# Routing tables of a two-layer MoE kernel: one-hot tables with the pair index innermost, in two-byte numbers, built on VectorE

## The chip, the cores and the metric

One core of a Trainium2 chip. Its engines run side by side, each with a queue of its own: TensorE (PE; PEld is its weight load), VectorE (DVE), ScalarE (ACT), GpSimd (POOL) and SyncE (SP, which here only issues DMAs). The metric is the device time of one launch in microseconds. Every stretch below is one core's.

## The reference, cut to what matters

The input is x of shape (4, 24, 16, 256): 1536 tokens of 256 numbers. There are two layers. Each adds an attention-like mixer to x, normalises the tokens, and adds a mixture of eight experts of which every token uses two. Layer 1 differs from layer 0 in its gates, width and activation.

```python
router = softmax(xf @ gate_w + gate_b)
k_scores, k_idx = top_k(router, 2)
comb = zeros((t, 8)).at[arange(t)[:, None], k_idx].add(k_scores)
for i in range(8):
    h = silu(xf @ w1[i] + b1[i])
    out = out + (h @ w2[i] + b2[i]) * comb[:, i:i + 1]
```

The kernel computes each expert only for the tokens that chose it, so it needs lists: which tokens go to which expert, and with which gate.

## The kernel before, in words

**Work and order.** Tokens lie in 12 tiles of 128 (token = tile x 128 + partition). A token and its first or second choice form a pair; each partition holds 24 pairs (PAIRS = 2 choices x 12 tiles). Per layer the order is: normalise, transpose, scores and values (the value products are in `values`, L1133, through `product`, L1097 to L1099; their weights are `xnT_hi` and `xnT_lo`, taken every 16th element), projection, second normalise, gates (`route`), the routing tables, and then a loop over blocks of 128 gathered token rows, 24 to 31 of them, each for one expert (`step`, L1306). Each engine has its own hand-written program; semaphores order them. PE runs filler matmuls in its waits (`keep_busy`, L1101).

**The routing tables.** DVE turns the gates into a slot number for each pair (L922 to L963). The slot's low seven bits are its row in a block (`rowblk[:, 0]`), the rest its block (`rowblk[:, 1]`); `rowblk` is four-byte. Then two one-hot tables are made:

- `blk_hot` (L967) has, for each pair, a one at its block out of TAB = 32. `onehot_blk` holds five products of it: with the token number within the tile (L972, DVE), with the tile's first token (L555, `blk_value` at L310, POOL) and with three parts of the gate (L590 on POOL for two of them, L1031 on DVE for the third).
- `onehot_row` (L976) has, for each pair, a one at its row out of 128. It takes one tensor_scalar for each of the 24 pairs, comparing `iota_bf` (0 to 127, two-byte) with that pair's row.

PE multiplies them, pair by pair, into PSUM: 24 matmuls of 64 columns give the token list (L1242), and 24 of 96 columns the gate list (L1324). The weights are a pair's 128 rows, the moving columns its blocks. In both tables the pair index is outside, so that a matmul reads packed numbers. PE starts the first list in four groups of six pairs (ROW_CHUNKS), each when DVE has made its six rows (`hot_rows`).

**What hangs on them.** From the first list DVE makes `gather_tab` (L983 to L985), POOL issues `gather(0)` (L571), and when the rows have landed PE transposes them (L1256), ACT and DVE split them in a high and a low part (L721, L1016), and PE makes `first_product(0)`. Behind that on PE come the 24 matmuls of the gate list, then `step(0)`. DVE meanwhile does the block arithmetic (L1034 to L1052), reads the gate list (L1056 to L1058) and enters its loop. POOL makes its two gate products between `gather(0)` and `gather(1)`. Between the first list and the first gathered block PE runs 12 fillers (BUSY_GATHER), before it 16 (BUSY_LIST).

**Memory.** `region_a` is used anew by each stage; during the tables `h_sb`, `hT_hi` and others share its place, since they are first written later. ACT's queue around the mixer's end is: copies of `outT` (L674), the cast of the biases (L680, waits for their load), a table load (L682), then the high parts of an expert's weights (L624) for POOL's subtractions (L544).

Of the kernel before, what the change touches and what calls it, by code (L numbers as in the profile page):

```python
# [15 lines left out]
BF16 = mybir.dt.bfloat16  # L16
I32 = mybir.dt.int32
ALU = mybir.AluOpType
# [3 lines left out]
P = 128  # L22
# [3 lines left out]
TILES = TOKENS // P  # L26
# [6 lines left out]
E, TOPK = 8, 2  # L33
PAIRS = TILES * TOPK
# [5 lines left out]
TAB = MAX_BLOCKS + MAX_BLOCKS % 2  # L40
ROW_CHUNKS = 4

# [23 lines left out]
class LayerSems:  # L66


    def __init__(self, sem, L):
# [46 lines left out]
        self.hot_blk = sem(f"hot_blk_{L}")  # L116
        self.tab_mm = sem(f"tab_mm_{L}")
# [29 lines left out]
def metaformer(nc, x, conv_w, ffn_w, out):  # L147

    with ExitStack() as ctx:
        def sb(name, shape, dt=F32):  # L150
            return ctx.enter_context(nc.sbuf_tensor(name, shape, dt))

        def sem(name):
            return ctx.enter_context(nc.semaphore(name))
# [13 lines left out]
        with nc.sbuf_tensor("onehot_blk", [P, PAIRS, 5, TAB], BF16) as onehot_blk:  # L168
            pass
# [3 lines left out]
        xT_lo = sb("xT_lo", [P, KC, P], F32R)  # L173
        h_sb = sb("h_sb", [P, 1024])
        blk_hot = sb("blk_hot", [P, PAIRS, TAB], BF16)
# [4 lines left out]
        onehot_row = sb("onehot_row", [P, PAIRS, P], BF16)  # L180
# [58 lines left out]
        rowblk = sb("rowblk", [P, 2, PAIRS])  # L239
# [28 lines left out]
        tile_first = sb("tile_first", [P, TILES])  # L268
        iota_bf = sb("iota_bf", [P, P], BF16)
# [38 lines left out]
        def blk_value(eng, v, value):  # L308

            return eng.tensor_tensor(onehot_blk[:, :, v, :].rearrange("p (k i) b -> p k i b", k=TOPK),  # L310
                                     blk_hot[:, :, :].rearrange("p (k i) b -> p k i b", k=TOPK),
                                     value.unsqueeze(3).to_broadcast([P, TOPK, TILES, TAB]), ALU.mult)
# [154 lines left out]
        def _(pool):  # L467
            cc = [0]

            def made(ins):  # L470
                cc[0] += 1
                ins.then_inc(made_seq, 1)
                pool.wait_ge(made_seq, cc[0])
# [21 lines left out]
            for L in range(2):  # L495
# [16 lines left out]
                for q in range(PIECES * SLOTS):  # L512
                    if L == 0 and q == PIECES:
# [10 lines left out]
                        made(pool.tensor_copy(tile_first[:, :], token_i[:, :]))  # L524
                        made(pool.iota(token_i[:, 0:1], pattern=[[0, 1]], base=1, channel_multiplier=1))
                        made(pool.tensor_copy(token_id[:, :], token_i[:, 0:1]))
                        made(pool.tensor_copy(iota_bf[:, :], iota_i[:, :]))
# [10 lines left out]
                    if q == 2 * PIECES:  # L538
# [14 lines left out]

                pool.wait_ge(s.blk_hot, 1)
                blk_value(nc.gpsimd, 1, tile_first[:, :].unsqueeze(1).to_broadcast([P, TOPK, TILES])  # L555
                          ).then_inc(s.hot_blk, 1)
                pool.wait_ge(s.hot_blk, 1)
# [30 lines left out]
                pool.wait_ge(s.blk_hot, 2)  # L588
                for v in range(2):
                    blk_value(nc.gpsimd, 2 + v, gate_part[:, v, :, :]).then_inc(s.hot_blk, 1)  # L590
                    pool.wait_ge(s.hot_blk, v + 2)
# [17 lines left out]
        def _(act):  # L609
            for L in range(2):  # L610
# [61 lines left out]
                for j in range(0, 8, 2):  # L672
                    act.wait_ge(s.oT_mm, j + 1)
                    nc.scalar.copy(outT[:, j // 4, :, 4 * (j % 4):4 * (j % 4) + 4].rearrange("p n q -> p q n"),  # L674
                                   bank[4 + j % 4][:, 0:4 * BN].rearrange("p (q n) -> p q n", q=4)).then_inc(s.o_act, 1)

# [90 lines left out]
        def _(dve):  # L767
            nc.vector.memset(busy_in[:, :], 0.0).then_inc(busy_ready, 1)
            for L in range(2):
# [165 lines left out]
                if L == 0:  # L935
# [31 lines left out]
                nc.vector.tensor_tensor(blk_hot[:, :, :],  # L967
                                        iota[:, 0:TAB].unsqueeze(1).to_broadcast([P, PAIRS, TAB]),
                                        rowblk[:, 1, :].unsqueeze(2).to_broadcast([P, PAIRS, TAB]),
                                        ALU.is_equal).then_inc(s.blk_hot, 1)  # L970
                dve.wait_ge(s.blk_hot, 1)
                nc.vector.tensor_scalar(onehot_blk[:, :, 0, :], blk_hot[:, :, :], token_id[:, :], None, ALU.mult  # L972
                                        ).then_inc(s.hot_rows, 1)
                dve.wait_ge(s.y_mm, 6)
                for j in range(PAIRS):
                    hot = nc.vector.tensor_scalar(onehot_row[:, j, :], iota_bf[:, :], rowblk[:, 0, j:j + 1], None,  # L976
                                                  ALU.is_equal)
                    if (j + 1) % (PAIRS // ROW_CHUNKS) == 0:
                        hot.then_inc(s.hot_rows, 1)
# [51 lines left out]
                blk_value(nc.vector, 4, gate_part[:, 2, :, :]).then_inc(s.hot_rows, 1)  # L1031


# [60 lines left out]
        def _(pe):  # L1094
# [16 lines left out]
            for L in range(2):  # L1111
# [126 lines left out]
                pe.wait_ge(s.hot_blk, 1)  # L1238
                for j in range(PAIRS):
                    if j % (PAIRS // ROW_CHUNKS) == 0:  # L1240
                        pe.wait_ge(s.hot_rows, j // (PAIRS // ROW_CHUNKS) + 2)
                    mm = pe.matmul(bank[5][:, 0:2 * TAB], onehot_row[:, j, :],  # L1242
                                   onehot_blk[:, j, 0:2, :].rearrange("p v b -> p (v b)"),
                                   start=(j == 0), stop=(j == PAIRS - 1))
# [76 lines left out]
                pe.wait_ge(s.hot_blk, 3)  # L1321
                pe.wait_ge(s.hot_rows, ROW_CHUNKS + 2)
                for j in range(PAIRS):
                    mm = pe.matmul(bank[6][:, 0:3 * TAB], onehot_row[:, j, :],  # L1324
                                   onehot_blk[:, j, 2:5, :].rearrange("p v b -> p (v b)"),
                                   start=(j == 0), stop=(j == PAIRS - 1))
# [39 lines left out]
```

## Time and profile before

| what | value |
|---|---|
| median of 3 runs | 665.55 us (664.88 to 667.18) |
| span of the profiled execution | 669.3 us; no other time of that execution is given |
| PE, DVE, ACT, POOL busy | 600.0, 339.2, 278.0, 283.5 us |
| DMA | 59.89 MB, mean 89 GB/s |
| mean granted clock of PE | 0.943 of full |

Busy time is what an engine spends in instructions, not how well it uses them. A line of a timeline gives the start, the time from the first start to the last end, the engine, the line of the kernel, the output, the inputs and a count. [...]

### The profile page before, as it was taken

How to read it: one execution, taken by the hardware profiler on the slowest of the kernel's cores; microseconds unless marked ns; L12 is line 12 of the kernel's file. 1: busy time of each engine (PE TensorE's matmuls, PEld its weight loads, DVE VectorE, ACT ScalarE, POOL GpSimd, SP SyncE). 2: the span in 40 equal slices, each digit the busy share in tenths (PEclk: the TensorE clock that was granted, in tenths of full speed). 3: DMA queues.
4: the chain of work that ended last, by engine and by line, in shares of the span. 5: the costliest groups of instructions: out<-in, count | busy, mean ns of one | idle time of the engine just before them, and what ended most of it. 6: DMA issues, size and time to landing. Idle time of an engine off the chain costs nothing.

```text
span 669.3 us, 15565 instructions
## 1 busy us (share of the span) xinstructions
PE 600.0 (90%) x3942; PEld 514.9 (77%) x3943; DVE 339.2 (51%) x745; ACT 278.0 (42%) x528; POOL 283.5 (42%) x309
## 2 busy tenths in 40 slices
PE   8898837999999999999869985689999999999992
PEld 4797614879888898897549774269999999999982
DVE  6635797454232643442186376744465555553330
ACT  5376522544333643443064736022344354432220
POOL 4948334254343434343354536223433543344332
PEclk9799968999999999999879996779999999999995
DMA  6423780264212521243203059302153552121111
GB/s 228 127 64 101 243 299 17 67 180 102 39 31 36 153 39 31 36 103 88 78 21 124 18 165 305 91 16 34 30 160 91 139 118 39 24 32 31 31 28 16
DMA packets 41418, 59.89 MB, mean 89 GB/s; under 512 B 5072, under 2 KB 34816, under 8 KB 41392
## 3 DMA queue, kind: packets, MB, share of 16 engines
q1 hardware_dynamic: 30448, 45.39, 21.4%
q0 software_dynamic: 10944, 14.17, 12.6%
q8 instruction: 14, 0.23, 0.2%
q14 instruction: 12, 0.10, 0.1%
HBM read 46.96 MB, written 13.63 MB: 91 GB/s over the span
## 4 chain that ended last, share of the span: by engine, by line
PE 74%; DVE 13%; DMA 4%; issue 4%; ACT 1%; DVEq 1%; ACTq 1%; POOL 0%; SPq 0%; POOLq 0%
PE bank L1097 17%; PE bank L1099 17%; PE bank L1098 17%; PE bank L1288 6%; PE bank L1273 4%; PE bank L1176 2%; PE bank L1256 2%; PE bank L1209 2%; DVE stats L780 2%; DVE onehot_row L976 2%; PE bank L1153 1%; PE bank L1198 1%; DMA expert_io<-xn_dram,gather_tab 1%; DMA xres<-in_x_dram 1%; PE bank L1105 1%
## 5 line engine op out<-in xcount | busy, mean ns | idle before, releaser
L1097 PE MATMUL bank<-w_hi,xT_hi 128*128 x336 | 139.7, 416 | 0.0
L1097 PE MATMUL bank<-w_hi,hT_hi 128*128 (+1 forms) x392 | 117.2, 299 | 5.9 <-DVE hT_lo L1069 5.9
L1099 PE MATMUL bank<-w_hi,xT_lo 128*128 x336 | 115.5, 344 | 0.0
L1098 PE MATMUL bank<-w_lo,xT_hi 128*128 x336 | 115.5, 344 | 0.0
L1098 PE MATMUL bank<-w_lo,hT_hi 128*128 (+1 forms) x392 | 112.2, 286 | 0.0
L1099 PE MATMUL bank<-w_hi,hT_lo 128*128 (+1 forms) x392 | 112.1, 286 | 0.0
L1069 DVE TENSOR_TENSOR hT_lo<-bank,hT_hi 128x512 fp32r<-128x512 f32 (+1 forms) x112 | 64.7, 619 | 63.8 <-ACT hT_hi L742 32.5
L742 ACT CAST hT_hi<-bank 128x512 fp32r<-128x512 f32 (+1 forms) x112 | 54.3, 536 | 99.0 <-PE bank L1288 98.9
L1097 PEld LDWEIGHTS bank<-w_hi,hT_hi 128*128 128x128 f32 (+1 forms) x392 | 76.4, 195 | 8.3 <-issue 7.6
L571 POOL DMA_INDIRECT expert_io<-xn_dram,gcol x58 | 59.0, 1017 | 47.2 <-POOL gcol L567 36.9
L544 POOL TENSOR_TENSOR w_lo<-raw,w_hi 128x1024 fp32r<-128x1024 f32 (+1 forms) x24 | 56.9, 2396 | 50.5 <-ACT w_hi L624 50.5
L1098 PEld LDWEIGHTS bank<-w_lo,hT_hi 128*128 128x128 f32 (+1 forms) x392 | 76.5, 195 | 0.0
L1099 PEld LDWEIGHTS bank<-w_hi,hT_lo 128*128 128x128 f32 (+1 forms) x392 | 76.5, 195 | 0.0
L582 POOL DMA_INDIRECT mid_dram<-expert_io,scol x28 | 44.8, 1601 | 72.4 <-DVE expert_io L1087 71.5
L1025 DVE TENSOR_TENSOR w_lo<-raw,w_hi x40 | 48.9, 1240 | 46.0 <-ACT w_hi L730 45.0
L582 POOL DMA_INDIRECT out_dram<-expert_io,scol x28 | 44.9, 1603 | 61.9 <-DVE expert_io L1087 59.9
L1097 PEld LDWEIGHTS bank<-w_hi,xT_hi 128*128 128x128 f32 x336 | 65.8, 196 | 3.3
L1099 PEld LDWEIGHTS bank<-w_hi,xT_lo 128*128 128x128 f32 x336 | 63.9, 190 | 4.8
L1098 PEld LDWEIGHTS bank<-w_lo,xT_hi 128*128 128x128 f32 x336 | 64.7, 193 | 3.8
L1273 PE MATMUL bank<-bias_rows,expert_sel 96*128 96x336 bf16 (+1 forms) x168 | 57.6, 343 | 3.0 <-DVE xT_lo L1016 3.0
L721 ACT CAST xT_hi<-bank 128x256 fp32r<-128x256 f32 x58 | 21.5, 370 | 93.2 <-PE bank L1256 93.1
L752 ACT ACTIVATE h_sb<-bank 128x512 f32<-128x512 f32 x56 | 33.6, 600 | 53.5 <-PE bank L1099 53.5
(200 smaller groups left out, 1030.8 us busy)
## 6 DMA issues: line engine op xcount, KB each, us to landing
raw<-in_L_ffn_w_dram SPq DMA_DIRECT2D x32, 512.0 KB, 4.1
raw<-in_L_ffn_W_dram SPq DMA_DIRECT2D x16, 672.0 KB, 4.0
raw<-in_L_ffn_W_dram SPq DMA_DIRECT2D x16, 336.0 KB, 4.6
xn_dram<-raw SPq DMA_DIRECT2D x6, 512.0 KB, 3.7
xres<-in_x_dram SPq DMA_DIRECT2D x3, 512.0 KB, 4.6
wqkv<-in_L_conv_W_qkv_dram SPq DMA_DIRECT2D x2, 768.0 KB, 7.4
mid_dram<-xres SPq DMA_DIRECT2D x3, 512.0 KB, 5.6
xres<-mid_dram SPq DMA_DIRECT2D x3, 512.0 KB, 4.9
```

What stands on the lines that cost most here:

```text
L544: pool.tensor_tensor(w_lo[:, e, at], raw[:, 0, at], w_hi[:, e, at].bitcast(F32), ALU.subtract).then_inc(s.pool_split, 1)
L571: pool.indirect_dma_start(out=xg, out_offset=None, in_=xn_dram, in_offset=bass.IndirectOffsetOnAxis(ap=rows, axis=0)).then_inc(s.gathered, 16)
L582: pool.indirect_dma_start(out=acc, out_offset=bass.IndirectOffsetOnAxis(ap=scol[:, :], axis=0), in_=y_sb, in_offset=None, bounds_check=TOK ...
L742: nc.scalar.copy(hT_hi[0:f.kh, half * j:half * (j + 1), :], bank[4 + j][0:f.kh, 0:half * P].rearrange("p (k s) -> p k s", s=P)).then_inc(s ...
L752: nc.scalar.activation(h_sb[:, f.chunk * j:f.chunk * (j + 1)], bank[j][:, 0:f.chunk], ACT.Silu).then_inc(s.h, 1)
L1025: nc.vector.tensor_tensor(w_lo[:, slot, at], raw[:, (q // PIECES) % 2, at], w_hi[:, slot, at].bitcast(F32), ALU.subtract).then_inc(s.w_lo, 1)
L1069: nc.vector.tensor_tensor(hT_lo[0:f.kh, part, :], bank[4 + j][0:f.kh, 0:half * P].rearrange("p (k s) -> p k s", s=P), hT_hi[0:f.kh, part, ...
L1097: pe.matmul(out, hi, w_high, start=first, stop=False)
L1098: pe.matmul(out, hi, w_low, start=False, stop=False)
L1099: return pe.matmul(out, lo, w_high, start=False, stop=last)
L1273: pe.matmul(bank[n][:, 0:f.chunk], expert_sel[:, e, :], bias_rows[:, cs], start=True, stop=False)
L1288: mm = pe.transpose(bank[4 + j][0:f.kh, k * P:(k + 1) * P], h_sb[:, o:o + f.kh], ident[:, :])
```

## The change

Both tables get the pair index innermost, and all compared and multiplied numbers two bytes. An `iota_rep` (each of 0 to 127, six times over) is written once per layer by ACT. It lies where `h_sb` lies later. The block table and the products run over 768 contiguous elements. `onehot_row` is made by four tensor_tensor operations of 128 x 6 elements instead of 24 tensor_scalar operations. All products of `blk_hot` move to DVE; those that POOL made, with its waits, go. The tile product stands ahead of the row tables on DVE, the three gate products stand together behind `xT_low(0)`. PE waits for both value products ahead of the first list, and for all five ahead of the second; the matmuls read one pair with a step of 6 elements (weights) or 24 (columns). The number of matmuls and their sizes stay.

```diff
+PER_CHUNK = PAIRS // ROW_CHUNKS
-        with nc.sbuf_tensor("onehot_blk", [P, PAIRS, 5, TAB], BF16) as onehot_blk:
+        with nc.sbuf_tensor("onehot_blk", [P, 5, TAB, PAIRS], BF16) as onehot_blk:
+        with nc.sbuf_tensor("iota_rep", [P, P, PER_CHUNK], BF16) as iota_rep:
+            pass
-        blk_hot = sb("blk_hot", [P, PAIRS, TAB], BF16)
+        blk_hot = sb("blk_hot", [P, TAB, PAIRS], BF16)
-        onehot_row = sb("onehot_row", [P, PAIRS, P], BF16)
+        onehot_row = sb("onehot_row", [P, ROW_CHUNKS, P, PER_CHUNK], BF16)
-        rowblk = sb("rowblk", [P, 2, PAIRS])
+        rowblk = sb("rowblk", [P, 2, PAIRS], BF16)
-        tile_first = sb("tile_first", [P, TILES])
-        iota_bf = sb("iota_bf", [P, P], BF16)
+        tile_first = sb("tile_first", [P, TOPK, TILES], BF16)
...
-            return eng.tensor_tensor(onehot_blk[:, :, v, :].rearrange("p (k i) b -> p k i b", k=TOPK),
-                                     blk_hot[:, :, :].rearrange("p (k i) b -> p k i b", k=TOPK),
-                                     value.unsqueeze(3).to_broadcast([P, TOPK, TILES, TAB]), ALU.mult)
+            return eng.tensor_tensor(onehot_blk[:, v, :, :], blk_hot[:, :, :],
+                                     value.unsqueeze(1).to_broadcast([P, TAB, PAIRS]), ALU.mult)
...
-                        made(pool.tensor_copy(tile_first[:, :], token_i[:, :]))
+                        for k in range(TOPK):
+                            made(pool.tensor_copy(tile_first[:, k, :], token_i[:, :]))
-                        made(pool.tensor_copy(iota_bf[:, :], iota_i[:, :]))
...
-                pool.wait_ge(s.blk_hot, 1)
-                blk_value(nc.gpsimd, 1, tile_first[:, :].unsqueeze(1).to_broadcast([P, TOPK, TILES])
-                          ).then_inc(s.hot_blk, 1)
-                pool.wait_ge(s.hot_blk, 1)
...
                 gather(0)
-                pool.wait_ge(s.blk_hot, 2)
-                for v in range(2):
-                    blk_value(nc.gpsimd, 2 + v, gate_part[:, v, :, :]).then_inc(s.hot_blk, 1)
-                    pool.wait_ge(s.hot_blk, v + 2)
                 gather(1)
...
+                if L == 0:
+                    act.wait_ge(const_done, 2)
+                nc.scalar.copy(iota_rep[:, :, :], iota[:, :].unsqueeze(2).to_broadcast([P, P, PER_CHUNK])
+                               ).then_inc(s.iota_in, 1)
                 act.wait_ge(s.bias_in, 6 * 16)
...
-                nc.vector.tensor_tensor(blk_hot[:, :, :],
-                                        iota[:, 0:TAB].unsqueeze(1).to_broadcast([P, PAIRS, TAB]),
-                                        rowblk[:, 1, :].unsqueeze(2).to_broadcast([P, PAIRS, TAB]),
+                dve.wait_ge(s.iota_in, 1)
+                nc.vector.tensor_tensor(blk_hot[:, :, :].rearrange("p b (c j) -> p b c j", c=ROW_CHUNKS),
+                                        iota_rep[:, 0:TAB, :].unsqueeze(2).to_broadcast([P, TAB, ROW_CHUNKS, PER_CHUNK]),
+                                        rowblk[:, 1, :].rearrange("p (c j) -> p c j", c=ROW_CHUNKS).unsqueeze(1)
+                                        .to_broadcast([P, TAB, ROW_CHUNKS, PER_CHUNK]),
                                         ALU.is_equal).then_inc(s.blk_hot, 1)
                 dve.wait_ge(s.blk_hot, 1)
-                nc.vector.tensor_scalar(onehot_blk[:, :, 0, :], blk_hot[:, :, :], token_id[:, :], None, ALU.mult
-                                        ).then_inc(s.hot_rows, 1)
+                nc.vector.tensor_scalar(onehot_blk[:, 0, :, :], blk_hot[:, :, :], token_id[:, :], None, ALU.mult
+                                        ).then_inc(s.hot_blk, 1)
+                blk_value(nc.vector, 1, tile_first[:, :, :].rearrange("p k i -> p (k i)")).then_inc(s.hot_blk, 1)
                 dve.wait_ge(s.y_mm, 6)
-                for j in range(PAIRS):
-                    hot = nc.vector.tensor_scalar(onehot_row[:, j, :], iota_bf[:, :], rowblk[:, 0, j:j + 1], None,
-                                                  ALU.is_equal)
-                    if (j + 1) % (PAIRS // ROW_CHUNKS) == 0:
-                        hot.then_inc(s.hot_rows, 1)
+                for c in range(ROW_CHUNKS):
+                    nc.vector.tensor_tensor(onehot_row[:, c, :, :], iota_rep[:, :, :],
+                                            rowblk[:, 0, c * PER_CHUNK:(c + 1) * PER_CHUNK].unsqueeze(1)
+                                            .to_broadcast([P, P, PER_CHUNK]), ALU.is_equal).then_inc(s.hot_rows, 1)
...
                 dve.wait_ge(s.blk_hot, 2)
-                blk_value(nc.vector, 4, gate_part[:, 2, :, :]).then_inc(s.hot_rows, 1)
+                for v in range(3):
+                    blk_value(nc.vector, 2 + v, gate_part[:, v, :, :].rearrange("p k i -> p (k i)")
+                              ).then_inc(s.hot_blk, 1)
...
-                pe.wait_ge(s.hot_blk, 1)
+                pe.wait_ge(s.hot_blk, 2)
                 for j in range(PAIRS):
-                    mm = pe.matmul(bank[5][:, 0:2 * TAB], onehot_row[:, j, :],
-                                   onehot_blk[:, j, 0:2, :].rearrange("p v b -> p (v b)"),
+                    mm = pe.matmul(bank[5][:, 0:2 * TAB], onehot_row[:, j // PER_CHUNK, :, j % PER_CHUNK],
+                                   onehot_blk[:, 0:2, :, j].rearrange("p v b -> p (v b)"),
                                    start=(j == 0), stop=(j == PAIRS - 1))
...
-                pe.wait_ge(s.hot_blk, 3)
-                pe.wait_ge(s.hot_rows, ROW_CHUNKS + 2)
+                pe.wait_ge(s.hot_blk, 5)
                 for j in range(PAIRS):
-                    mm = pe.matmul(bank[6][:, 0:3 * TAB], onehot_row[:, j, :],
-                                   onehot_blk[:, j, 2:5, :].rearrange("p v b -> p (v b)"),
+                    mm = pe.matmul(bank[6][:, 0:3 * TAB], onehot_row[:, j // PER_CHUNK, :, j % PER_CHUNK],
+                                   onehot_blk[:, 2:5, :, j].rearrange("p v b -> p (v b)"),
                                    start=(j == 0), stop=(j == PAIRS - 1))
```

## Rows read from the trace of the kernel before

**Rows 1.** The page, busy tenths in 40 slices of the span: PE.

```profile
PE   8898837999999999999869985689999999999992
```

**Rows 2.** Windows, busy us of each engine; last: granted clock, DMA share, GB/s.

```profile
core 0: us, PE busy (x) PEld busy (x) DVE busy (x) ACT busy (x) POOL busy (x), PEclk, DMA share, GB/s
115.30:334.00 218.70, 212.33 (x1392) 183.28 (x1392) 84.48 (x134) 90.81 (x158) 87.38 (x114) 0.99 0.32 74
95.30:102.43 7.13, 2.90 (x32) 1.55 (x30) 6.50 (x26) 0.00 (x0) 1.65 (x1) 0.94 0.33 111
```

**Rows 3.** The chain of waits in layer 0 from 94.4: start us, us, what.

```profile
95.30 0.97 DVE blk_hot L967
96.30 0.42 DVE onehot_blk L972
96.72 5.13 DVE onehot_row L976 x24
...
102.43 0.20 DVE id_sb L983
...
104.00 2.92 DMA expert_io<-xn_dram,gather_tab
```

**Rows 4.** Timelines of DVE and POOL around the first table; brackets: idle before, releaser.

```profile
96.63 5.21 DVE L976 TENSOR_SCALAR onehot_row<-iota_bf,rowblk 128x128 bf16<-128x128 bf16 x24
...
96.40 1.65 POOL L310 TENSOR_TENSOR onehot_blk<-blk_hot,tile_first 128x768 bf16<-128x768 bf16 x1 [7.99 <-DVE blk_hot L967]
...
429.21 0.19 DVE L983 TENSOR_SCALAR id_sb<-bank 128x32 f32<-128x32 f32 x1 [0.44 <-PE bank L1242]
...
436.43 0.95 DVE L310 TENSOR_TENSOR onehot_blk<-blk_hot,gate_part 128x768 bf16<-128x768 bf16 x1
```

**Rows 5.** Single lines of DVE: ns min/median/max, first and last start, forms.

```profile
L967 DVE TENSOR_TENSOR blk_hot<-iota,rowblk x2: 957/958/959, 95.3 to 422.2; 128x768 bf16<-128x768 f32 x2
...
L972 DVE TENSOR_SCALAR onehot_blk<-blk_hot,token_id x2: 420/420/420, 96.3 to 423.2; 128x768 bf16<-128x768 bf16 x2
...
L957 DVE TENSOR_TENSOR expert_io<-place,pick x2: 357/358/358, 93.5 to 420.5; 128x192 f32<-128x192 f32 x2
```

**Rows 6.** Timelines of PE (layer 1, gate list) and PEld (value products; packed loads).

```profile
443.93 1.20 PE L1324 MATMUL bank<-onehot_blk,onehot_row 128*128 128x96 bf16 x24
444.98 0.41 PE L1256 MATMUL bank<-ident,expert_io 128*128 128x128 f32 x2
...
30.00 0.26 PEld L1099 LDWEIGHTS bank<-wv,w_lo 128*96 128x96 f32 x1
...
32.02 0.26 PEld L1099 LDWEIGHTS bank<-wv,w_lo 128*96 128x96 f32 x1
...
46.35 0.72 PEld L1167 LDWEIGHTS bank<-ident,region_a 96*96 96x96 f32 x8 [0.65 <-issue]
```

**Rows 7.** Windows around the first gather, in layer 0 and in layer 1.

```profile
98.10:101.50 3.40, 1.03 (x18) 0.70 (x18) 3.40 (x23) 0.00 (x0) 0.00 (x0) 1.00 0.00 0
...
432.40:435.90 3.50, 1.49 (x6) 0.45 (x4) 0.22 (x2) 0.22 (x1) 3.02 (x3) 0.96 0.16 42
436.76:442.70 5.94, 5.94 (x21) 5.24 (x21) 3.82 (x14) 1.68 (x3) 1.44 (x1) 0.50 0.08 22
```

**Rows 8.** Timeline of PE in layer 0: fillers, then the gate list.

```profile
102.21 4.13 PE L1105 MATMUL bank<-busy_in 128*128 128x512 bf16 x12
...
111.86 1.20 PE L1324 MATMUL bank<-onehot_blk,onehot_row 128*128 128x96 bf16 x24
```

**Rows 9.** Timeline of DVE around the second table, layer 0 and layer 1.

```profile
108.24 1.73 DVE L310 TENSOR_TENSOR onehot_blk<-blk_hot,gate_part 128x768 bf16<-128x768 bf16 x1
...
113.69 0.19 DVE L1056 COPY id_sb<-bank 128x32 f32<-128x32 f32 x1
...
445.23 0.19 DVE L1056 COPY id_sb<-bank 128x32 f32<-128x32 f32 x1 [4.23 <-PE bank L1324]
```

**Rows 10.** Timeline of ACT after the mixer in layer 0.

```profile
58.36 1.53 ACT L680 CAST bias_rows<-region_d 96x1600 bf16<-96x1600 f32 x1
...
65.62 0.20 ACT L615 ACTIVATE std<-mean_var 128x4 f32<-128x4 f32 x1 [3.26 <-DVE mean_var L788]
```

More of the change, by code:

```diff
@@ L116, in __init__ @@
         self.hot_blk = sem(f"hot_blk_{L}")
+        self.iota_in = sem(f"iota_in_{L}")
         self.tab_mm = sem(f"tab_mm_{L}")
@@ L1237, in _ @@
                 keep_busy(BUSY_LIST, 0)
-                pe.wait_ge(s.hot_blk, 1)
+                pe.wait_ge(s.hot_blk, 2)
                 for j in range(PAIRS):
-                    if j % (PAIRS // ROW_CHUNKS) == 0:
-                        pe.wait_ge(s.hot_rows, j // (PAIRS // ROW_CHUNKS) + 2)
-                    mm = pe.matmul(bank[5][:, 0:2 * TAB], onehot_row[:, j, :],
-                                   onehot_blk[:, j, 0:2, :].rearrange("p v b -> p (v b)"),
+                    if j % PER_CHUNK == 0:
+                        pe.wait_ge(s.hot_rows, j // PER_CHUNK + 1)
+                    mm = pe.matmul(bank[5][:, 0:2 * TAB], onehot_row[:, j // PER_CHUNK, :, j % PER_CHUNK],
+                                   onehot_blk[:, 0:2, :, j].rearrange("p v b -> p (v b)"),
                                    start=(j == 0), stop=(j == PAIRS - 1))
```

## The prediction

> **What bounds the kernel now.** I read the page first: in its 40 slices PE is busy nine or ten tenths nearly everywhere in the second half of each layer [rows 1]. The windows explain the dips. From 115.30 to 334.00, an expert loop, PE is busy for 212.33 of 218.70 us; the change puts nothing in there. In the 7.13 us from 95.30 to 102.43, where the first table is made, PE works 2.90 and DVE 6.50 [rows 2]. The chain of waits names the links of that stretch: blk_hot, the token product, 24 row operations (5.13 us, the longest), six matmuls, the gather list at 102.43, then 2.92 us of DMA [rows 3]. Layer 1 repeats it from 422.2 [rows 5] to 429.21 [rows 4]. So the first table stands on the path in both layers, and the PE-bound loops start earlier by what it saves. The profiled span is 669.3 us; the record gives its execution no other time. It lies 3.75 above the median of 665.55; I sum against the span and take the difference to the median. A measurement can tell about 0.3%, 2.0 us, from no change.
>
> **DVE, first table.** The 24 row operations last 5.21 us, although POOL's tile product (96.40, 1.65 us) runs into the first ones [rows 4]. Neighbours without a wait overlap: the first row operation starts at 96.63 [rows 4], 0.09 before the token product ends [rows 3]. After the change nothing runs on POOL here, and DVE has the block table, the token product, the tile product and four row tables, of 768 elements each. The token product stays at 0.42 us. The other six are tensor_tensor on 768 elements. Upper end for one: 0.958, the block table of before; lower end: 0.420, the one-input product of the same size [rows 5]. A tensor_tensor on 192 elements takes 0.358 [rows 5], so the kind costs 1.04 ns an element on a fixed 0.16 us; the one-input two-byte product, on the same fixed part, 0.34 ns. In the old layout a per-pair value stood still along the inner axis, and L310 in layer 1, all two-byte, took 0.95 [rows 4], no less than with four-byte input. The new layout gives every operand a moving inner run of two-byte numbers. I take half the base cost, between these ends: 0.16 + 0.40 = 0.56 us, the next one starting 0.48 later. [...]
>
> From the start of blk_hot: token product at 0.60, tile product at 0.93, row tables at 1.41, 1.89, 2.37 and 2.85, the last done at 3.41.
>
> **PE, first table.** In exchange PE reads its weights 12 bytes apart and its columns 48 bytes apart. Packed, 24 such matmuls start within 444.98 - 443.93 us, 0.044 each: the lower end [rows 6]. The only rows with scattered weights are the value products, 96 elements 64 bytes apart: they start 0.168 us apart (twelve intervals from 30.00 to 32.02) and load for 0.26, while packed 96-column loads run 8 in 0.72, 0.090 each [rows 6]. Scattering costs them a factor of 1.9. That 0.168, for 128 columns instead of 96, is 0.224: the upper end. I scale the packed pace, 0.044 x 1.9 = 0.083 us, nearer to the lower end because these are two-byte weights, as in its row, and 12 bytes scatter less than 64. PE starts when the first row table is done, at 2.02, and at 0.083 (0.50 a group of six) just keeps up. Before, 0.59 us lay between the last row operation (101.84) and id_sb (102.43); with 6 x 0.044 in it, the fixed part is 0.33. So id_sb starts at 3.41 + 0.33 + 0.50 = 4.24, against 7.13 and 7.0. **Saved: 2.9 and 2.75 us.**
>
> [...]
>
> **The clock in layer 0.** The twelve filler matmuls behind the table run mostly at the low level and take 4.13 us, to 106.34 [rows 8]; before them PE worked 1.03 of 3.40 us [rows 7]. With less idling before them I expect them at the full clock, 2.6 us, done near 102. The gathered rows land at 106.92 - 2.9 = 104.0. PE then idles about two us where it idled 0.6. In layer 1 such a gap (busy 1.49 of 3.50 us) was followed by 5.94 us at 0.50 [rows 7]. [...] I take 2.9 us of it, half of what layer 1 shows, because more work precedes it; half of that is lost, **1.45 us**. In layer 1 the slow stretch is there already; I count it unchanged.
>
> **The second table.** Its 24 matmuls last 1.20 us [rows 6]; at 0.083 they last 2.15, 0.95 more. In layer 1 DVE already waited 4.23 us for them [rows 9]: **0.95 lost**. In layer 0 PE ended them at 111.86 + 1.20 = 113.06 [rows 8], but DVE came to read at 113.69, held by its block arithmetic [rows 9]; 0.6 is covered, 0.35 lost. All three gate products now run on DVE, 3 x 0.48 = 1.44 us ahead of that arithmetic. In layer 0 the single one took 1.73 beside POOL's two [rows 9], so the arithmetic is slightly early; in layer 1 it is 0.6 late, inside the 4.23. PE waits for all three before these matmuls, behind its first product, which lasts longer than they do; past that cover they would delay PE one for one. POOL's second gather moves ahead by its two products, but the next step hangs on the gate table: nothing gained.
>
> **The rest.** ACT gets one copy of 768 elements per layer, ahead of the bias cast, whose 1600 take 1.53; so it costs less than that, about 0.8. ACT later stands idle for 3.26 us before 65.62 [rows 10], which covers it. The cast releases subtractions on POOL, which end shortly before DVE normalises; if they now collide, a few tenths of a us a layer. The copy's new wait for POOL's constants is met long before: the bias load that ACT waits for next was itself held for them; DVE's wait for the copy comes 30 us after it. No DMA is added, removed or moved on SP; the gathers of POOL keep their order.
>
> **Sum.** Layer 0: 2.9 - 1.45 - 0.35 = 1.1. Layer 1: 2.75 - 0.95 = 1.8. Together 2.9: span 666.4, time 662.7 us.
>
> **Rivals.**
> - *PE's scattered reads become the bound (slower).* Above 0.083 us every matmul lengthens both streams in both layers, 96 matmuls. The gain is gone at 0.083 + 2.9 / 96 = 0.113, and the loss measurable from 0.134. For it: the value products' own pace, and columns scattered too. Against: the small step and size. At 0.168 it costs 96 x 0.085 = 8.2: 670.9. At 0.224, 13.5, less the clock loss, which then vanishes: 674.8.
> - *DVE stays at the base rate.* Six operations of 0.96, spaced 0.88: the last row table ends at 5.81, id_sb starts at 6.64. Saved 0.5 and 0.35; the second table loses 0.95 in layer 1 and about 1.0 in layer 0, where three products replace one. Together 1.1 worse: 666.7. For it: inner runs of only six elements. Against: all operands two-byte and moving.
> - *No clock loss in layer 0*: 1.45 better, 661.2.
> - *Scattered reads cost nothing*: 0.24 a layer at the first table, 1.3 in all at the second: 660.9; with the clock kept too, 659.5.
>
> **How the numbers follow.** Forecast 0.40, no clock loss 0.08, free reads 0.08, PE bound 0.24, DVE at the base rate 0.15, a table that comes off the path to no effect 0.05. Faster: nine tenths of the forecast and the two better cases, 0.52. Slower: three quarters of PE's rival, which lie above 0.134, and a fifth of the others that are no gain, 0.25 with the forecast's worst tail. Same: 0.23. The range reaches from the free reads with the clock kept, 659.5, to a pace of 0.154, 669.5; about 0.13 lies above and 0.05 below.
>
> **What would show it.** Right: blk_hot, tile product and row tables of 0.56 us; table matmuls 0.08 us apart; id_sb 4.2 us after blk_hot; fillers of layer 0 in 2.6 us, its first product at half clock. Wrong: DVE operations of 0.96, or 24 matmuls that take over 2.7 us.

## The result and the profile after

The changed kernel takes 675.09 us (median of 4 runs, 671.48 to 679.55) against 666.37 for the kernel before (4 runs beside it, 664.88 to 667.43): ratio 1.0121, 95% interval [1.0082, 1.0159]. It is slower; 662.7 was forecast, and the range ended at 669.5. A second measurement of both, `control_after` and `control_before` below, gives 1.0114 and 1.0007. The ratios here are those on record; the quotient of two medians can lie up to 0.3% from them (in this measurement it is 1.0131). Slow executions enter no ratio below: three of six of `before_delay` and two of twelve of `before_two_fillers` (774 to 3258 us), and one of `after_two_fillers` (679.6).

The profiled execution of the changed kernel has a span of 673.7 us. Its line numbers differ a little: L976 is now L978, L983 is L984, L310 is L313, L1056 is L1057, L1105 is L1106, L1256 is L1257, and the list matmuls stay at L1243 and L1324. First DVE's timeline in layer 0; it answers to [rows 4, 5, 9].

```profile
93.38 0.56 DVE L967 TENSOR_TENSOR blk_hot<-iota_rep,rowblk 128x768 bf16<-128x768 bf16 x1
93.98 0.42 DVE L973 TENSOR_SCALAR onehot_blk<-blk_hot,token_id 128x768 bf16<-128x768 bf16 x1
94.31 0.55 DVE L313 TENSOR_TENSOR onehot_blk<-blk_hot,tile_first 128x768 bf16<-128x768 bf16 x1
94.78 1.96 DVE L978 TENSOR_TENSOR onehot_row<-iota_rep,rowblk 128x768 bf16<-128x768 bf16 x4
98.46 0.19 DVE L984 TENSOR_SCALAR id_sb<-bank 128x32 f32<-128x32 f32 x1 [1.72 <-PE bank L1243]
...
104.48 1.49 DVE L313 TENSOR_TENSOR onehot_blk<-blk_hot,gate_part 128x768 bf16<-128x768 bf16 x3
...
114.90 0.19 DVE L1057 COPY id_sb<-bank 128x32 f32<-128x32 f32 x1 [5.32 <-PE bank L1324]
```

DVE does what was asked of it: the row table is finished 3.36 us after blk_hot begins (94.78 + 1.96 - 93.38). But it then waits 1.72 us for PE, and 5.32 us at the second table, where it waited for nothing before [rows 9]. PE's timeline of the same stretch, which answers to [rows 6, 8]:

```profile
95.48 2.94 PE L1243 MATMUL bank<-onehot_blk,onehot_row 128*128 128x64 bf16 x24 [0.69 <-DVE onehot_row L978]
98.25 2.77 PE L1106 MATMUL bank<-busy_in 128*128 128x512 bf16 x12
103.06 0.58 PE L1257 MATMUL bank<-ident,expert_io 128*128 128x128 f32 x2 [2.05 <-DMA expert_io<-xn_dram,gather_tab]
...
105.65 0.63 PE L1099 MATMUL bank<-w_lo,xT_hi 128*128 x1
...
110.47 4.32 PE L1324 MATMUL bank<-onehot_blk,onehot_row 128*128 128x96 bf16 x24
```

The chain of waits of that stretch, which answers to [rows 3]: the table matmuls are now its two long links.

```profile
95.48 2.96 PE bank L1243 x24
...
100.03 2.99 DMA expert_io<-xn_dram,gather_tab
...
110.63 4.17 PE bank L1324 x24
```

The lines that touch the row table, in ns (min/median/max):

```profile
L1243 PEld LDWEIGHTS bank<-onehot_blk,onehot_row x48: 124/126/143, 95.4 to 431.7; 128*128 128x128 bf16 x48
L1243 PE MATMUL bank<-onehot_blk,onehot_row x48: 275/294/301, 95.5 to 431.8; 128*128 128x64 bf16 x48
L1324 PEld LDWEIGHTS bank<-onehot_blk,onehot_row x48: 124/126/147, 110.5 to 447.6; 128*128 128x128 bf16 x48
L1324 PE MATMUL bank<-onehot_blk,onehot_row x48: 347/352/355, 110.5 to 447.8; 128*128 128x96 bf16 x48
L978 DVE TENSOR_TENSOR onehot_row<-iota_rep,rowblk x8: 550/551/553, 94.8 to 429.8; 128x768 bf16<-128x768 bf16 x8
```

A group's length less its last matmul, over 23 intervals, is the pace: (2.94 - 0.29) / 23 = 0.115 us for 64 columns, (4.32 - 0.35) / 23 = 0.173 for 96. Both are **1.80 ns a column**: what is paid is the number of columns, not the number of matmuls. Before, 96 columns went at 0.044 [rows 6].

Windows of the changed kernel, with PEclk, the granted clock as a share of full speed, behind the engines. The first answers to [rows 2]; then the first product of layer 0, and a stretch of the mixer of layer 1, which the diff touches only by a copy on ACT.

```profile
core 0: us, PE busy (x) PEld busy (x) DVE busy (x) ACT busy (x) POOL busy (x), PEclk, DMA share, GB/s
116.49:325.50 209.01, 203.20 (x1351) 179.05 (x1349) 83.75 (x131) 90.79 (x158) 83.78 (x111) 0.99 0.32 73
...
105.40:111.00 5.60, 5.60 (x18) 3.85 (x17) 3.77 (x15) 1.34 (x3) 0.49 (x1) 0.58 0.09 23
352.00:360.00 8.00, 8.00 (x42) 6.57 (x41) 5.78 (x7) 0.00 (x0) 8.00 (x4) 0.57 0.25 88
```

The last one in the kernel before:

```profile
352.00:360.00 8.00, 8.00 (x58) 7.20 (x57) 6.99 (x7) 2.11 (x4) 7.03 (x3) 1.00 0.38 114
```

So there are two sources: longer table matmuls, and stretches in which the granted clock is at its lower level (0.58 and 0.57 in these windows). To place them I cut each span at the same six events, read from the timelines (us; the columns add up to the spans):

| stretch | before | control_before | after | control_after | cols_packed | after_fillers | packed_split_fillers |
|---|---|---|---|---|---|---|---|
| start to blk_hot, layer 0 | 95.30 | 94.44 | 93.38 | 93.34 | 95.47 | 93.88 | 97.18 |
| to the lower part of block 1 (xT_lo) | 19.99 | 19.97 | 23.11 | 23.03 | 18.51 | 20.60 | 18.48 |
| expert loop, to the 50 fillers | 209.42 | 210.52 | 209.03 | 209.24 | 212.26 | 210.15 | 209.74 |
| mixer, to blk_hot of layer 1 | 97.52 | 97.47 | 101.53 | 101.27 | 99.72 | 97.06 | 96.93 |
| to xT_lo of block 1 | 25.29 | 21.11 | 23.45 | 25.19 | 21.34 | 22.15 | 18.88 |
| to the end | 221.78 | 221.29 | 223.20 | 222.63 | 220.80 | 223.46 | 220.59 |
| span | 669.3 | 664.8 | 673.7 | 674.7 | 668.1 | 667.3 | 661.8 |

Mean of the two changed records less mean of the two old ones: tables of layer 0 +3.1, mixer of layer 1 +3.9, its tables +1.1, the rest +1.4, the first two stretches without tables -1.5 and -0.8. Together 7.2; the medians of the two controls lie 8.7 apart. These are single executions. The first stretch shows their scatter: it ran from 92.67 to 96.52 us in the seven records of kernels with the old layouts, whose code is the same up to there. So of the six differences the -1.5 and the -0.8 mean nothing by themselves, and the +1.4 little.

### The profile page after: what moved, and what is told of

It is laid out like the page before. It is cut to its first block, busy times and chain, and to the rows that moved or that the text cites. A ratio compares the mean times of both kernels' runs of the same rounds, so it can differ in the third digit from the quotient of the medians.

```text
span 673.7 us, 15525 instructions
## 1 busy us (share of the span) xinstructions
PE 610.0 (91%) x3942; PEld 525.8 (78%) x3943; DVE 332.5 (49%) x711; ACT 279.4 (41%) x530; POOL 273.3 (41%) x303
## 4 chain that ended last, share of the span: by engine, by line
PE 78%; DVE 12%; issue 3%; DMA 2%; ACT 1%; DVEq 1%; ACTq 1%; POOL 0%; POOLq 0%
PE bank L1098 18%; PE bank L1099 17%; PE bank L1100 17%; PE bank L1289 6%; PE bank L1274 5%; PE bank L1177 2%; DVE stats L779 2%; PE bank L1257 2%; PE bank L1210 2%; PE bank L1154 1%; PE bank L1324 1%; PE bank L1199 1%; PE bank L1106 1%; DVE pick L926 1%; DVE region_b L876 1%
```

## Experiments

Theory: the scattered reads of PE cost the time, and of them the moving columns. Rivals: the scattered weights, the move of POOL's products to DVE, and a fall of the clock. Every kernel was measured against runs of the kernel before on its own chip, whose medians lay between 666.4 and 667.8 us.

**Both kernels again.** No edit.

> The kernel before, unchanged, as a control and for a second profile. Both theories: ratio 1.00. Open: whether the slow first gather of layer 1 (4.46 us) and the stretches at the low clock sit where they sat in the first profile. If the difference between kernels is partly the clock's luck, stretches at 0.50 move between executions, and time goes with the mean granted clock.

> The changed kernel, unchanged, on the same chip. Ratio about 1.012. Theory 1 (scattered columns): both streams of table matmuls keep a pace of 1.80 ns a column (0.115 and 0.173 us), id_sb about 5.1 us after blk_hot, 24 gate-list matmuls over 4.1 us. Theory 2 (clock's luck): times scatter by several us with the mean granted clock, more than those of the kernel before.

Measured: 666.95 us, ratio 1.0007 [0.9978, 1.0036], and 675.69 us, 1.0114 [1.0076, 1.0152]. The time of a run goes, by and large, with its mean granted clock: among those of `control_after`, 0.940 came with 678.7 us and 0.951 with 672.1.

**Packed columns.** The changed kernel with the block table in its old order; the row table stays in the new one.

```diff
-        with nc.sbuf_tensor("onehot_blk", [P, 5, TAB, PAIRS], BF16) as onehot_blk:
+        with nc.sbuf_tensor("onehot_blk", [P, PAIRS, 5, TAB], BF16) as onehot_blk:
...
-                                   onehot_blk[:, 2:5, :, j].rearrange("p v b -> p (v b)"),
+                                   onehot_blk[:, j, 2:5, :].rearrange("p v b -> p (v b)"),
```

> The changed kernel with the block table and its products laid out as before (a pair's blocks packed), the row table as changed: weights stay scattered, columns are packed. If scattered columns set the pace: 24 gate-list matmuls in at most 1.6 us (at most 0.06 each) instead of 4.3, about 2.8 us per layer less; DVE's block operations go back to 0.95 us, 0.8 us more ahead of the row tables, id_sb about 4.9 us after blk_hot; the kernel falls below the changed one by some 6 us and at or a little below the kernel before. If scattered weights set the pace: the streams keep 0.115 and 0.173 us a matmul, and the time stays or rises by 1.6 us.

Measured: 669.32 us, 1.0022 [0.9996, 1.0047]. Timeline of PE, and the lines of its matmuls:

```profile
109.67 1.32 PE L1323 MATMUL bank<-onehot_blk,onehot_row 128*128 128x96 bf16 x24
...
L1323 PEld LDWEIGHTS bank<-onehot_blk,onehot_row x48: 125/130/147, 109.7 to 444.7; 128*128 128x128 bf16 x48
L1323 PE MATMUL bank<-onehot_blk,onehot_row x48: 209/210/248, 109.7 to 444.7; 128*128 128x96 bf16 x48
```

The pace is (1.32 - 0.21) / 23 = 0.048 us, with the weights still 12 bytes apart. So the moving columns set it, and scattered weights add about 0.004 us. The time falls by 0.92% of the kernel before, 6.1 us. It isn't below that kernel's, although its table stretch in layer 0 is 1.5 us shorter and that of layer 1 no longer (21.34 us against 25.29 and 21.11): the loop of layer 0 takes 212.26 us instead of 209.4 to 210.5, and the mixer of layer 1 takes 99.72 instead of 97.5. About 1.5 us of the loop is taken up below; the rest stays open.

**Packed weights.** The other half: the row table in the old order, by 24 operations, with one more cast on DVE; columns scattered.

```diff
-        onehot_row = sb("onehot_row", [P, ROW_CHUNKS, P, PER_CHUNK], BF16)
+        onehot_row = sb("onehot_row", [P, PAIRS, P], BF16)
```

> The changed kernel with the row table made and laid out as before (24 row operations, a pair's rows packed), the block tables as changed: columns stay scattered, weights are packed. If scattered columns set the pace: gate-list matmuls stay at 0.17 us each, 24 in 4.2; id_sb comes about 6.4 us after blk_hot, so 1.3 us per layer slower than the changed kernel. If scattered weights set it: 24 in 1.2 us, about 3 us per layer less at the second table, and the kernel about 3 us faster than the changed one.

Measured: 674.99 us, 1.0123 [1.0085, 1.0161], with

```profile
441.07 4.23 PE L1329 MATMUL bank<-onehot_blk,onehot_row 128*128 128x96 bf16 x24
```

Packed weights give back 0.09 us of a group of 24. The first rival falls. This kernel was expected 2.6 us slower than the changed one, since id_sb comes later (6.32 us after blk_hot); the ratios, 1.0123 and 1.0114, can't tell that from no difference. In its record the fillers behind the first table last until shortly before the rows (PE idles 0.46 us in layer 0 and not at all in layer 1), and both first products run at the full clock, 3.36 and 4.55 us.

**The kernel before with all products on DVE.** Old layouts; POOL's three products a layer go to DVE.

```diff
-                pool.wait_ge(s.blk_hot, 1)
-                blk_value(nc.gpsimd, 1, tile_first[:, :].unsqueeze(1).to_broadcast([P, TOPK, TILES])
-                          ).then_inc(s.hot_blk, 1)
...
+                blk_value(nc.vector, 1, tile_first[:, :].unsqueeze(1).to_broadcast([P, TOPK, TILES])
+                          ).then_inc(s.hot_blk, 1)
```

> The kernel before with all five products of the block table on DVE, both layouts as before (products at 0.95 us, 24 row operations). POOL's collision gone: row operations 24 in 4.0 us instead of 5.2, but the tile product adds 0.88 ahead of them, so id_sb about 6.8 us after blk_hot instead of 7.1. Three gate products 2.6 us instead of 1.7 in layer 0, where they hold the block arithmetic: 0.9 later there less 0.3; layer 1 covered. In all within 1 us of the kernel before: moving the products is not what cost the time. A rival that blames DVE's extra work: 3 us or more slower.

Measured: 668.58 us, 1.0024 [0.9995, 1.0052]. Timeline of DVE:

```profile
94.00 0.95 DVE L310 TENSOR_TENSOR onehot_blk<-blk_hot,tile_first 128x768 bf16<-128x768 bf16 x1
94.86 3.98 DVE L970 TENSOR_SCALAR onehot_row<-iota_bf,rowblk 128x128 bf16<-128x128 bf16 x24
99.29 0.19 DVE L977 TENSOR_SCALAR id_sb<-bank 128x32 f32<-128x32 f32 x1 [0.44 <-PE bank L1238]
```

The 24 row operations take 3.98 us without POOL beside them, and 5.21 with it [rows 4]. id_sb comes 6.62 us after blk_hot begins instead of 7.13, although DVE has one product more. The move alone costs 0.0 to 0.5%; it isn't the 1.1%.

**A delay alone.** In the kernel before the 24 gate-list matmuls are issued four times over, with the same result: 4.25 us instead of 1.20, columns and weights packed.

```diff
+                for t in range(4):
+                    for j in range(PAIRS):
```

> The kernel before with the 24 packed gate-list matmuls issued four times over, so that the stream lasts 4.3 us as in the changed kernel; tables, layouts and engines as before. If a delay at this place passes straight through: layer 1 loses 3.15 us, layer 0 3.15 less the 0.6 covered by DVE, 5.7 us in all (ratio 1.0086). If a shift of this size also moves later stretches into the low clock level (the mixer of layer 1 took 86.8 us in the changed kernel and 83.6 before): 7 to 9 us, and its mixer shows the low level in the scores.

Measured, from three executions: ratio 1.013 [1.0075, 1.0184], a loss of 5.0 to 12.3 us. The record has 2.64 us more in the table stretch of layer 0 (22.63) and 3.1 more than `control_before` in that of layer 1 (24.23). So in this record 3.05 us of PE work lengthen each table stretch by nearly their whole length, although every operand is packed, and twice that is most of the loss.

**More fillers behind the first table.** PE idled 2.05 us ahead of the gathered rows. BUSY_GATHER goes from 12 to 20, in three kernels: the changed one, the one with packed columns, and the one before.

```diff
-BUSY_LOAD, BUSY_POOL, BUSY_NORM, BUSY_TOP, BUSY_LIST, BUSY_GATHER, BUSY_LAYER = 32, 8, 10, 4, 16, 12, 50
+BUSY_LOAD, BUSY_POOL, BUSY_NORM, BUSY_TOP, BUSY_LIST, BUSY_GATHER, BUSY_LAYER = 32, 8, 10, 4, 16, 20, 50
```

> The changed kernel with 20 fillers instead of 12 behind the token list (nothing else). In the changed kernel the 12 run at the full clock in 2.8 us and PE then idles 2.0 us before the gathered rows. If that idling drops the clock in the first product of layer 0: the 20 fillers last 4.4 us, end just before the rows, the first product of layer 0 (5.65 us from its start to the gate list) returns to 3.3 us, and the time falls by 2.3 us, more if layer 1 follows (5.8 to 7.2 us there, 4.1 at the full clock). If the clock falls for another reason: no change, or up to 2 us slower where fillers run at the low level. The table matmuls keep 0.115 and 0.173 us.

Measured: 671.78 us, 1.0067 [1.0041, 1.0093].

```profile
98.73 4.50 PE L1106 MATMUL bank<-busy_in 128*128 128x512 bf16 x20
103.50 0.44 PE L1257 MATMUL bank<-ident,expert_io 128*128 128x128 f32 x2 [0.27 <-DMA expert_io<-xn_dram,gather_tab]
...
106.19 0.40 PE L1098 MATMUL bank<-w_hi,xT_hi 128*128 x1
...
108.50 4.29 PE L1324 MATMUL bank<-onehot_blk,onehot_row 128*128 128x96 bf16 x24
```

With the gap filled the first product runs at 0.40 us a matmul instead of 0.63, and its stretch falls from 5.65 us to 3.38; the table matmuls stay at 4.29. The idle gap that the quicker first table leaves favours the low clock, but doesn't decide it alone. In layer 0 of `cols_packed` the same gap stands, and the first product behind it runs at the full clock (1.00); in layer 1 of the same record it runs at 0.58:

```profile
104.77 0.44 PE L1256 MATMUL bank<-ident,expert_io 128*128 128x128 f32 x2 [2.04 <-DMA expert_io<-xn_dram,gather_tab]
...
106.91 0.40 PE L1098 MATMUL bank<-w_lo,xT_hi 128*128 x1
...
434.99 0.44 PE L1256 MATMUL bank<-ident,expert_io 128*128 128x128 f32 x2 [1.76 <-DMA expert_io<-xn_dram,gather_tab]
```

The 17 records have 34 such places. At eight of them PE idled 1.71 to 2.06 us ahead of the rows, and six of these first products ran in part or wholly at the low level (granted clock 0.54 to 0.73); at the other 26 it idled 0.63 us at most, and one did (layer 0 of `after_two_fillers`, 0.66). What else decides was not settled.

> Row table as changed, block tables packed as before, 20 fillers instead of 12 behind the token list. Gains 2.4 us at the first table of each layer, loses 0.1 at the second. If idling before the first product is what costs the clock: no stretch at the low level in the first product of either layer (3.3 and 4.1 us), which saves 2.9 us in layer 1 against the same kernel with 12 fillers (669.3): about 664 to 666 us, at or below the kernel before. If the clock follows something else: as with 12 fillers or slower.

> The kernel before with 20 fillers instead of 12 behind the first table, as in the changed kernel that came out at 1.0067 with them (1.0114 without). Theory: they cover the idling ahead of the first products here too; layer 0 is unchanged (its first product is at full clock already), layer 1's first product runs at full clock in every execution: 1 to 3 us better, ratio 0.996 to 0.999. Rival: the fillers themselves delay the gather's transposes: ratio over 1.000.

Measured: 668.45 us, 1.0001 [0.9970, 1.0032], and 669.34 us, 0.9998 [0.9970, 1.0026]. The kernel before gains nothing: in layer 0 its gathered rows are transposed 12.61 us after blk_hot begins instead of 11.67, because the 20 fillers, which last 5.87 us there, stand in their way. With packed columns the next gap shows, behind the transposes of the first block. PE waits 2.56 us there in `cols_packed` too, and from the xT_lo of block 1 to the next it takes 6.61 and 6.63 us in these two records, where the two records of the kernel before take 5.05 and 5.08. In `cols_packed_fillers` the loop of layer 0 opens with

```profile
114.02 0.39 PE L1273 MATMUL bank<-bias_rows,expert_sel 96*128 96x512 bf16 x1 [2.56 <-DVE xT_lo L1016]
...
115.81 0.63 PE L1099 MATMUL bank<-w_hi,xT_lo 128*128 x1
```

**Fillers in that gap too.** Ten behind the transposes of block 0, in both layers (six where the columns are scattered).

```diff
                     h_transpose(b)
+                    if isinstance(b, int) and b == 0:
+                        keep_busy(10, 0)
                     first_product(b + 1, e_new)
```

> The changed kernel with its block table in the old layout (packed columns), 20 fillers behind the first table instead of 12, and 10 new fillers on PE between the transposes of the first block's product and the first product of block 1, where PE idled 2.56 us in the same kernel without them and where the loop of layer 0 then opened at a lower clock (matmuls of 0.60 to 0.65 us instead of 0.40). Theory: what the faster first table saves is given back through those low stretches; then the loops open at full clock (0.40 us), about 1.5 us per layer are saved against the kernel without the new fillers, and the time is about 665.5 us, ratio near 0.996 of before. Rival: the clock falls elsewhere instead, or the loop waits for its weights anyway; then the ratio stays at 1.000.

> The kernel before with 20 fillers behind the first table and the 10 new ones ahead of block 1's first product. Theory: another 1.5 us less than with the first set alone, only in layer 1, where a low stretch lies there in some executions: ratio about 0.995. If it equals the changed version with packed columns and the same fillers, the packed change's table gain of 2.4 us a layer does not reach the end; if that one is lower by 2 to 4 us, it does.

> The changed kernel, scattered columns, with 20 fillers behind the first table and 6 ahead of block 1's first product, where PE idled 1.28 us. Theory: the matmuls at 1.80 ns a column still cost about 3 us a layer at the second table, and only the clock is repaired: 1 us or less better than with 20 fillers alone, ratio about 1.005. Rival: with the clock repaired everywhere the scattered columns cost nothing: ratio below 1.000.

Measured: 668.24 us, 0.9990 [0.9964, 1.0016]; 1.0046 [1.0017, 1.0076]; 675.13 us, 1.0091 [1.0061, 1.0122]. All three came out above what the theory gave. The timeline of PE in layer 1 of `packed_two_fillers` says why:

```profile
442.14 0.40 PE L1256 MATMUL bank<-ident,expert_io 128*128 128x128 f32 x2
444.43 0.95 PE L1288 MATMUL bank<-ident,h_sb 128*112 128x128 f32 x6 [1.88 <-DVE h_sb L1077]
445.21 2.32 PE L1105 MATMUL bank<-busy_in 128*128 128x512 bf16 x10
```

In layer 1 the gap lies ahead of the block's transposes, not behind them: the fillers stand on the path there, and block 1 takes 7.8 us from one xT_lo to the next, all of it at the full clock. Without them it takes 5.9 at the full clock (`cols_packed`) and 7.4 where the clock fell to 0.77 (`cols_packed_fillers`): they cost more than they save. The fault was in the experiment, so it was put right.

**Fillers where each layer idles.** Packed columns, 20 fillers behind the first table; in layer 0 ten behind the transposes, in layer 1 eight ahead of them. The kernel before and the changed one get the eight in layer 1 (the changed one the 20 as well).

```diff
+                    if isinstance(b, int) and b == 0 and L == 1:
+                        keep_busy(8, 5)
                     h_transpose(b)
+                    if isinstance(b, int) and b == 0 and L == 0:
+                        keep_busy(10, 0)
```

> Changed kernel, block table packed, 20 fillers behind the first table; in layer 0, 10 fillers behind the first block's transposes (PE idled 2.56 us there); in layer 1, 8 fillers ahead of them, where PE idled 1.88 us. Theory: the gain of the table is given back through low clock at the start of the loops; with both gaps filled, the loop of layer 1 has no block interval over 6.0 us at its start and both loops open with 0.40-us matmuls: 2 us less than packed_two_fillers, about 666 us, ratio 0.996 (0.994 to 0.998). Rival: the clock falls elsewhere and takes the same time: ratio 0.999 to 1.001.

> The kernel before with 8 fillers ahead of the first block's transposes in layer 1, where PE idled 1.81 us, and nothing else. Theory: the low stretch near the start of the loop of layer 1 was there in its records; at best 1 us is saved: ratio 0.998 to 1.000. Rival: the fillers stand in the way by more than they save: over 1.001.

> The changed kernel, scattered columns, 20 fillers behind the first table, 8 ahead of the first block's transposes in layer 1. Theory: about 1 us less than with the 20 alone (1.0067): 1.005; the 3 us by which the scattered columns lengthen each second table remain. Rival, all of the loss is clock: below 1.001.

Measured: **665.69 us, 0.9965 [0.9942, 0.9988]**; 666.57 us, 0.9992 [0.9966, 1.0018]; 670.13 us, 1.0052 [1.0021, 1.0084]. The first lies where the theory put it (0.996), the others too (0.998 to 1.000, and 1.005). In `packed_split_fillers`:

```profile
113.63 2.32 PE L1105 MATMUL bank<-busy_in 128*128 128x512 bf16 x10
116.34 0.39 PE L1273 MATMUL bank<-bias_rows,expert_sel 96*128 96x512 bf16 x1 [0.39 <-DVE xT_lo L1016]
...
117.78 0.40 PE L1099 MATMUL bank<-w_hi,xT_lo 128*128 x1
...
438.89 1.89 PE L1105 MATMUL bank<-busy_in 128*128 128x512 bf16 x8
440.93 0.95 PE L1288 MATMUL bank<-ident,h_sb 128*112 128x128 f32 x6
```

Both loops open at the full clock, and the time is 3.6 us below `cols_packed`. This version beats both kernels: the kernel before by 0.1 to 0.6%, the changed one by more than 1%. That it beats the kernel before with its own eight fillers isn't shown, since the intervals overlap. The scattered columns remain a loss with most of the clock mended: 1.0052. Not all of it is, for in the record of `after_split_fillers` the eight fillers themselves last 3.32 us instead of 1.89, at a granted clock of 0.54.

## Why the prediction was wrong

**The step that failed is the term "0.044 x 1.9 = 0.083 us" for a table matmul.** It was scaled from the packed pace and put near the lower end, because the weights lie only 12 bytes apart. The runs show that the weights were the wrong operand to look at: with their scattering alone the pace is 0.048, with the columns' 0.173, and for 64 columns 0.115. The rows for the upper end, 0.168 to 0.224 [rows 6], held the value for 96 columns, though their own scattered operand was the weights, so that this agreement is luck. Priced anew, the 48 matmuls of the first lists cost 48 x (0.115 - 0.083) = 1.5 us more than forecast and the 48 of the gate lists 48 x (0.173 - 0.083) = 4.3, together 5.9. So this term alone turns the forecast from 662.7 into 668.6. `cols_packed` confirms the operand and the size, though not this very sum: it gives back 6.1 us with the pace at 0.048, its block operations at 0.95 again and its own low stretches.

It is the columns, 48 bytes apart, that cost: 4.32 us a group of 24 in the changed kernel. For weights 12 bytes apart this case shows next to no price: with packed columns their load takes 130 ns (`cols_packed`) against 98 where they are packed too (the kernel before), and the group 1.32 us against 1.20.

The stretches place the rest. The two table stretches were forecast 2.9 us shorter and came out 4.2 longer (3.1 and 1.1). Of these 7.1 us the pace is 5.9 and the clock of layer 0, below, 0.95. Outside the tables, where the prediction changed nothing, they sum to 3.0, above all the 3.9 of the mixer of layer 1; the medians lie 1.5 us further apart than the records and show no place for it.

Point by point:

- *DVE, first table*: right. 0.56 was forecast for each tensor_tensor, 0.55 to 0.56 measured; the row table was due at 3.41 and came at 3.36. That forecast took half of 0.80 us beside the fixed 0.16, the author's estimate between 0.420 and 0.958: no row of the kernel before shows a tensor_tensor at that rate. The runs show 0.55 us even with inner runs of six elements. The rival "base rate" falls.
- *id_sb*: 4.24 forecast, 5.08 and 5.06 measured; saved 2.05 and 1.92 instead of 2.9 and 2.75. PE no longer keeps up with DVE. The 0.84 is the pace term again.
- *Clock of layer 0*: the order of events was as forecast (fillers at full clock, 2.77 us for 2.6; then an idle gap of 2.05 for "about two"; then the first product at the low level, a granted clock of 0.54 from 104.82 to 110.47), the loss larger. From that product to the gate list it takes 5.65 us instead of 3.28: 2.4 lost for 1.45 forecast. That the product was spared half of the slow stretch was a choice without a row behind it. Both records of the changed kernel have the low stretch, but that of `cols_packed`, with the same gap, hasn't.
- *Clock of layer 1, counted unchanged*: no. The record of before showed a slow first product [rows 7], the second record of the same kernel didn't (4.46 us from there to the gate list, 7.17 in the first). One execution isn't enough to say that a slow stretch is always there.
- *Second table*: 0.95 forecast, 3.12 measured (4.32 - 1.20). The cover in layer 0, the 0.6 us by which DVE came late [rows 9], was a fifth of it; DVE waited 5.32 us.
- *ACT and POOL*: ACT's copy took 0.83 to 0.84 us for about 0.8, and neither it nor POOL's subtractions stand in the new chain of the tables. Of the mixer's +3.9 us in layer 1 the windows show the clock (0.57 where it was 1.00). The same stretch at the low level stands in the records of `cols_packed`, `before_all_dve` and `before_split_fillers`, and not in those of `after_fillers` and `packed_split_fillers`: it belongs to no one layout. Eight of the 17 records have it (granted clock 0.50 to 0.61 from 352 to 360, against 1.00 in the other nine), both of the changed kernel among them and neither of the kernel before. What decides on it was not settled, nor how much of the 3.9 us the change brings in every execution.
- *Rival "PE's scattered reads become the bound"*: this is what happened. It had the right sign and mechanism and was given 0.24. Its 670.9 took 0.168 for all 96 matmuls; the 48 of the gate lists had 0.173, but the 48 of the first lists 0.115, so that its 8.2 us should have been 5.9. From 668.6 the measured time is 6.5 us off: the clock of layer 0, which cost 2.4 and not 1.45, and what lies outside the tables, the mixer of layer 1 above all, which no step of the prediction had.

## What to carry to other kernels

A layout has readers as well as a writer. Before an inner axis is turned for one engine, count the elements that every other engine reads from the table, times its price for a scattered one, which on PE was 1.80 ns a moving column: here the first list came 2.4 us earlier a layer at best (id_sb 4.71 us after blk_hot in `cols_packed`), and PE paid for 24 x (64 + 96) columns. Turn only the table whose reader hardly pays; here that is the weights (0.048 us a matmul for 0.044).

What is saved ahead of PE leaves a gap, and the work behind the gap may then run at the low clock: here it did, in part or wholly, at six places of eight (granted clock 0.54 to 0.73). In layer 0 of the changed kernel that cost 2.4 us, where id_sb came 2.05 earlier. Look for the new gap in the timeline, layer by layer, and fill it with work that ends before the wait does.

## What the hardware showed that was not expected

- Moving columns of two bytes, 48 bytes apart, cost PE 1.80 ns each (0.115 us at 64, 0.173 at 96); packed, 24 matmuls of 96 columns go at 0.044 to 0.048 us.
- Behind an idle gap of 1.7 to 2.1 us the next product ran wholly or in part at the low level at six places of eight, behind one of 0.63 us or less at one of 26.
- Weights of two bytes, 12 bytes apart, cost next to nothing: 0.048 us a matmul with them, 0.044 without [rows 6].
- POOL's single tensor_tensor of 1.65 us beside DVE's row operations made these last 5.21 us instead of 3.98 (`before_all_dve`) and 3.99 (`weights_packed`): DVE lost 1.2 us by it.
- Eight more fillers, 1.7 us of useless work, made the changed kernel 0.5% faster; in the kernel before they changed nothing (0.9998).
